# One-hots of the dot attention's edges made during propagation, in halves, beside those of its nodes

## The chip, the cores and the metric

The kernel runs on one core of a Trainium2 chip. The time is that of one execution on the device, in microseconds (us). Engines are called as in the profile: PE (TensorE, matrix products; PEld is its weight load), DVE (VectorE), ACT (ScalarE), POOL (GpSimd) and SP (SyncE, which here only issues DMAs). ACT issues DMAs too.

## What is computed

Four graph layers over one graph of 3125 nodes with 96 features and 50000 edges, each fed with a layer norm and a ReLU and added to x. Cut to what matters:

```python
edge_index = jnp.stack([src, dst])
h = relu(layernorm(x))
x = x + L0(h, edge_index)      # propagation, K = 10: out = spmm(out) * 0.9 + h * 0.1
h = relu(layernorm(x))
x = x + L1(h, W, ...)          # graph attention (softmax over the edges of a node)
h = relu(layernorm(x))
x = x + L2(h, qW, kW, vW, src, dst)   # dot attention
h = relu(layernorm(x))
x = x + L3(h, edge_index, W, b)       # mean of neighbours, projected

# L0: out[row] = sum over edges of out[col] / sqrt(deg_row * deg_col), ten times
# L2, the dot attention, heads = 4:
q = (embeds[rows] @ qW); k = (embeds[cols] @ kW); v = (embeds[cols] @ vW)
scores = clip(sum over a head's features of q * k, -10, 10)
w = exp(scores) / (sum of exp over the edges of a row + 1e-8)
res = segment_sum(w * v, rows)
```

## The kernel before

Nodes lie in 25 tiles of 128 (`TILES`, padded length `NPAD` = 3200). Edges are bucketed by (tile of the source, tile of the target), and one bucket of 128 slots holds each pair, so 25 x 25 buckets are gone through once (one round).

**Stages.** `build_counts` counts the edges into a 25 x 25 matrix of 128 x 128 blocks (`count16`, on chip) and writes the edges' ids to DRAM in several layouts: `ids_dram` (slot by slot), `by_src` and `by_dst` (rows of ids). `propagate` is L0, `graph_attention` L1, `dot_attention` L2, `mean_aggregate` L3. They run one after the other, with a barrier between blocks.

**Propagation.** Ten turns (`K_STEPS`). In a turn, PE makes 25 sums (one for each tile i), each of 25 products of 128 x 128 by 128 x 192 (L1248), into five banks in rotation (`BANKS`). DVE turns each sum into the next turn's operand with the four instructions of `update` (L1171, L1173, L1175, L1177) and counts `y_ready` up. PE may start the sum of tile i + 5 when tile i has been updated, and the first sum of a turn needs the last tile of the turn before only for its last product. Before, `update` keeps its 32-bit result in `y32`, a quarter of the tensor `work`.

**Node one-hots on the side.** The dot attention gathers and scatters by matrix products with one-hot matrices. Those of the edges' source and target *within their tile's row of ids* (SRC and DST, "node one-hots", 2 x 25 of 128 x 3200 in f16) are made during propagation: 100 halves of 128 x 1600. For each, SP broadcasts a row of ids to all 128 partitions (L1029), DVE compares it in place with the partition's number (L1035), and ACT stores it to the DRAM tensor `hot_by_src` (L1040). There are three buffers in x. DVE makes one after the updates of tiles 1, 3, ..., 19 of each turn (`SPOT_AFTER`). After every fourth half SP also writes a tile of `count16` to DRAM (L1196).

**The dot attention's loop.** 25 steps s (source tiles), each of three groups of 10, 10 and 5 buckets, numbered j = 0 to 74. Each engine runs a program of its own, in a fixed order, and semaphores tie them together. Per group j, PE gathers q and k (`gather`, L1852 and L1853), the v of group j-1, and scatters group j-3 (L1881, L1882). k has one place in PSUM, so PE may gather the next k only when DVE's product of this one (L1941) is done. DVE does the product (L1941), the weighted value of group j-1 (L1948), which waits for ACT's three instructions of the weight of that group (L1906, L1908, L1910), and the reduction (L1954). Behind the reduction of a step's second group stands `spot_edges(s + 1)` (L1926): one instruction over 128 x 3200 that makes the next step's edge one-hot, the scatter matrix, from a table of slot ids (`cols`), and behind it `add` (L1932). SP loads the two node one-hots of step s three steps ahead (L1756), waiting for `q_done` and `v_done`.

## Time and profile before

| | us |
|---|---|
| median of 3 runs | 1625.02 (1624.86 to 1630.6) |
| profiled execution, its own time | 1627.73 |
| its span, first to last instruction | 1625.9 |
| DVE busy / PE busy / ACT busy / POOL busy | 1259.8 / 1237.4 / 546.2 / 373.9 |
| propagation, first to last sum | 324.65 to 859 |
| dot attention's loop, first to last product (L1941) | 1252.8 to 1518.0 |

The busy share of an engine over the whole span says little here, since stages with different limits follow each other: in the 40 slices of the page PE stands at 9 tenths through propagation with DVE at 5 to 8, and in the dot attention's slices DVE stands at 9 with PE at 8. The views that matter are the sums over a stretch and the timeline of one step. A row of the timeline gives the start, the duration, and in brackets how long the engine had been idle before it and what ended that. Two instructions that follow each other on DVE overlap by up to 0.1 us in their records, so what one costs is read from start to start.

### The profile page before, as it was taken

To read this page: it belongs to the slowest core of one execution; us is meant where nothing else is said; L and a number is where in the kernel's file an instruction comes from. 1 tells how busy PE (TensorE), PEld (TensorE's weight loads), DVE (VectorE), ACT (ScalarE), POOL (GpSimd) and SP (SyncE) were. 2 spreads that over 40 slices of the span, in tenths; PEclk is the share of its full clock that TensorE was granted. 3 is DMA by queue.
4 is the path that set the end of the run, shared out by engine and by line. 5 is a ranking of instruction groups with operands and counts; after the bars stand their busy time and mean duration, and the time that the engine had idled before them with its cause. 6 is when DMAs were issued, how large, how long until landed. Compare 5 with 4: busy or idle time off the path is not lost. (4 is left out here: it accounts for less than half of the span.)

```text
span 1625.9 us, 44876 instructions
## 1 busy us (share of the span) xinstructions
PE 1237.4 (76%) x18543; PEld 1174.0 (72%) x18544; DVE 1259.8 (77%) x2302; ACT 546.2 (34%) x1096; POOL 373.9 (23%) x211
## 2 busy tenths in 40 slices
PE   4767777399999999999994004888856888888468
PEld 3356767399899999999993004787755887888368
DVE  7888888766566565665667998999988999999733
ACT  0047777400000000000002873333335777777311
POOL 1400000000000000000001012888862665656300
PEclk6858777699999999999997556999997999999789
DMA  0012222375475565654563683555513444543293
GB/s 10 0 46 109 105 103 109 109 249 190 151 240 204 161 196 194 213 194 164 203 213 110 225 298 123 204 201 189 200 68 117 144 159 149 164 146 122 96 343 101
DMA packets 74936, 256.85 MB, mean 158 GB/s; under 512 B 17999, under 2 KB 19576, under 8 KB 74732
## 3 DMA queue, kind: packets, MB, share of 16 engines
q1 hardware_dynamic: 59996, 211.70, 38.6%
q10 hardware_dynamic: 14400, 40.97, 6.5%
q8 instruction: 160, 2.62, 0.7%
q0 software_dynamic: 336, 1.20, 0.3%
q14 instruction: 44, 0.36, 0.1%
HBM read 168.15 MB, written 85.68 MB: 156 GB/s over the span
## 5 line engine op out<-in xcount | busy, mean ns | idle before, releaser
L1248 PE MATMUL psum<-work,count 128*128 128x192 f16 x6250 | 521.4, 247 | 30.7 <-issue 30.7
L1248 PEld LDWEIGHTS psum<-work,count 128*128 128x128 f16 x6250 | 519.7, 98 | 32.5 <-issue 31.8
L1171 DVE SCALAR_TENSOR_TENSOR work<-psum,small,work 128x96 f32<-128x96 f32 x250 | 79.5, 318 | 177.4 <-PE psum L1248 177.3
L1585 PE MATMUL psum<-count 128*128 128x98 f16 x625 | 113.1, 209 | 134.5 <-DVE count L1632 98.2
L1852 PE MATMUL psum<-count 128*128 128x100 f16 (+1 forms) x1875 | 181.4, 207 | 44.5 <-DVE count L1941 30.7
L1852 PEld LDWEIGHTS psum<-count 128*128 128x128 f16 x1875 | 162.7, 98 | 55.3 <-issue 36.0
L929 ACT ACTIVATE work<-work 128x1248 f32<-128x1248 f32 (+1 forms) x6 | 7.2, 1203 | 576.9 <-DVE work L912 576.8
L1917 POOL TENSOR_TENSOR count<-count 128x1000 bf16<-128x1000 f32 (+1 forms) x75 | 160.8, 2143 | 122.0 <-ACT count L1901 122.0
L1624 POOL TENSOR_TENSOR count<-count 128x970 bf16<-128x970 f32 (+1 forms) x75 | 166.7, 2236 | 91.2 <-ACT count L1617 91.2
L1853 PE MATMUL psum<-count 128*128 128x100 f16 (+1 forms) x1875 | 180.8, 207 | 0.0
L1853 PEld LDWEIGHTS psum<-count 128*128 128x128 f16 x1875 | 164.4, 98 | 0.0
L1585 PEld LDWEIGHTS psum<-count 128*128 128x128 f16 x625 | 61.1, 98 | 141.1 <-DVE count L1632 98.4
L1214 POOL MEMSET x<- 128x96 f32 x1 | 0.2, 178 | 562.0 <-DMA onehots_by_src<-x 562.0
L1586 PE MATMUL psum<-count 128*128 128x98 f16 x625 | 112.9, 208 | 0.0
L1588 PE MATMUL psum<-count 128*128 128x98 f16 x625 | 112.8, 208 | 0.0
L1587 PE MATMUL psum<-count 128*128 128x98 f16 x625 | 112.7, 208 | 0.0
L1617 ACT CAST count<-count 128x970 f16<-128x970 f32 (+1 forms) x75 | 64.9, 867 | 110.3 <-DVE count L1668 110.3
L1536 DVE CUSTOM_DVE_ANT_0 count<-count 128x3200 bf16<-128x3200 f32 x25 | 91.0, 3641 | 4.8 <-ACT count L1386 0.8
L728 ACT ACTIVATE count<-psum 128x512 f32 (+3 forms) x175 | 92.8, 547 | 1.2 <-PE psum L458 1.2
L1632 DVE TENSOR_SCALAR count<-count,small 128x3200 f16<-128x3200 f16 x50 | 89.0, 1783 | 0.7 <-PEq L1484 0.7
L1173 DVE SCALAR_TENSOR_TENSOR work<-psum,small,work 128x96 f32<-128x96 f32 x250 | 79.4, 317 | 8.8
L2176 PE MATMUL psum<-count 128*128 128x194 f16 x625 | 58.4, 250 | 31.3 <-issue 31.3
(286 smaller groups left out, 2695.7 us busy)
## 6 DMA issues: line engine op xcount, KB each, us to landing
x<-bucket_rows_by_src SPq DMA_DIRECT2D x100, 400.0 KB, 4.6
onehots_by_src<-x ACTq DMA_DIRECT2D x100, 400.0 KB, 4.3
count<-bucket_rows_by_dst SPq DMA_DIRECT2D x50, 800.0 KB, 4.4
count<-onehots_by_src SPq DMA_DIRECT2D x50, 800.0 KB, 4.3
count_f<-count SPq DMA_DIRECT2D x25, 800.0 KB, 6.8
count<-count_turned SPq DMA_DIRECT2D x25, 800.0 KB, 5.8
count<-count_f SPq DMA_DIRECT2D x17, 800.0 KB, 4.3
count_turned<-x SPq DMA_DIRECT2D x25, 416.0 KB, 2.4
```

What stands on the lines that cost most here:

```text
L728: nc.scalar.activation(count16[:, bass.ds(t, 1), b0 * P:(b0 + n) * P], ps[:, at * CH:at * CH + n * P].unsqueeze(1), ACT.Copy, accum_out=in ...
L1248: last = nc.tensor.matmul(bank[i % BANKS], count16[:, j, i * P:(i + 1) * P], y[par][:, j, :], start=(j == 0), stop=(j == TILES - 1))
L1536: nc.vector.tensor_tensor_reduce(bent, asrc, masks[t % 2], 1.0, -3e38, ALU.subtract, ALU.max, top[:, t:t + 1]).then_inc(topped, 1)
L1585: nc.tensor.matmul(ps[:, at:at + GW], node_hot[SRC][t % 2][:, s, :], high[:, s, :], start=True, stop=False, skip_group_check=True)
L1586: nc.tensor.matmul(ps[:, at:at + GW], node_hot[SRC][t % 2][:, s, :], low[:, s, :], start=False, stop=False, skip_group_check=True)
L1587: nc.tensor.matmul(ps[:, at:at + GW], node_hot[DST][t % 2][:, s, :], wide_high[:, t, :], start=False, stop=False, skip_group_check=True)
L1588: last = nc.tensor.matmul(ps[:, at:at + GW], node_hot[DST][t % 2][:, s, :], wide_low[:, t, :], start=False, stop=True, skip_group_check=True)
L1624: nc.gpsimd.tensor_tensor(value_low[i % (LAG + 1)][:, 0:n * EW], value[i % RING][:, 0:n * EW], value_high[i % (LAG + 1)][:, 0:n * EW], ALU ...
L1632: nc.vector.tensor_scalar(node_hot[v][t % 2].rearrange("p t n -> p (t n)"), spread[v][t % 2], small[:, 504:505], None, ALU.is_equal).then_ ...
L1852: nc.tensor.matmul(slot(b, i, width), hot[:, t0 + i, :], high[:, of, at:at + width], start=True, stop=False, skip_group_check=True)
L1853: last = nc.tensor.matmul(slot(b, i, width), hot[:, t0 + i, :], low[:, of, at:at + width], start=False, stop=True, skip_group_check=True)
L1917: nc.gpsimd.tensor_tensor(value_low[i % 3][:, 0:n * VW], value[i % 2][:, 0:n * VW], value_high[i % 3][:, 0:n * VW], ALU.subtract).then_inc ...
```

## The change

The edge one-hots are no longer made inside the dot attention. They are made in propagation too, as 50 halves of 13 and 12 tiles (128 x 1664 and 128 x 1536), stored to DRAM behind the node one-hots (`hot_by_src` grows from 50 to 75 rows), and loaded from there in the dot attention as a third 800 KB load per step. So propagation has 150 pieces (`PIECES`), in the order node, edge, node (`piece % 3 == 1` is an edge piece), and they are made in the first nine turns: after the updates of tiles 1 to 20, in five of every six places. Node halves have four buffers in place of three, the fourth in the memory of `y32`; edge pieces have one, there too, and so an edge compare waits for the store of the edge piece before it. `update` keeps its 32-bit result in two small buffers (`passing`) but in the last turn, where it goes to `y32` as before. The table of slot ids is loaded once at propagation's start, only its source half (128 x 25 runs of 50 ids), ahead of the first node half on SP's queue, and POOL makes the row of numbers that it is compared with. Eleven semaphores of `build_counts` are cleared and given back to make room. The `cols` tensor and its load go from the dot attention.

```diff
-    spots, HALVES = m["spots"], BY_SRC_HALVES
-    SPOT_AFTER = range(1, 21, 2)
-    halves = [view(m["x"], i * HALF_ROW // 2, HALF_ROW, F16) for i in range(3)]
+    spots, steps_space, x_space = m["spots"], Space(m["work"][:, 3 * W:4 * W]), Space(m["x"])
+    node_halves = [x_space.take(HALF_ROW, F16) for _ in range(NODE_BUFFERS - 1)] + [steps_space.take(HALF_ROW, F16)]
+    pieces = Pieces(node_halves, steps_space.take(HALF_TILES[0][1] * P, F16), steps_space.take(2 * TILES * TILES, F16), view(m["small"], 160, P, F16))
+    passing = [steps_space.take(D), m["work"][:, 4 * W + P:4 * W + P + D]]
+    LAST = K_STEPS - 1
...
-            spots.loads(sp, halves, half_row, HALVES, store_count_tile)
+            spots.load_ids(sp, pieces, 0, ids_dram)
+            for n in range(NODE_HALVES):
+                spots.load(sp, pieces, 0, n, by_src)
+                store_count_tile(n)
...
                 for turn in range(K_STEPS):
+                    if turn == LAST:
+                        spots.wait_stored(dve)
                     for i in range(TILES):
-                        update(dve, turn * TILES + i, bank[i % BANKS], at_tile(i), y[1 - turn % 2])
-                        if i in SPOT_AFTER:
-                            spots.compare(dve, halves, turn * len(SPOT_AFTER) + SPOT_AFTER.index(i))
+                        update(dve, turn * TILES + i, bank[i % BANKS], at_tile(i), y[1 - turn % 2], y32[:, i, :] if turn == LAST else passing[i % 2])
+                        q = 20 * turn + i - 1
+                        if turn < LAST and 1 <= i <= 20 and q % 6 < 5:
+                            spots.compare(dve, pieces, 5 * (q // 6) + q % 6)
...
+    def compare_edges(self, dve, pieces, e):
+        s, half = divmod(e, 2)
+        t0, t1 = HALF_TILES[half]
+        if e == 0:
+            dve.wait_ge(self.counted, 1)
+            dve.wait_ge(self.ids_loaded, 16)
+        else:
+            dve.wait_ge(self.edges_stored, 16 * e)
+        shape = [P, t1 - t0, P // 2, 2]
+        self.nc.vector.tensor_tensor(pieces.edge[:, 0:(t1 - t0) * P].rearrange("p (t n d) -> p t n d", n=P // 2, d=2),
...
             def _(sp):
                 for s in range(3, TILES):
-                    for v, done in ((SRC, "q_done"), (DST, "v_done")):
+                    for v, done in ((SRC, "q_done"), (DST, "v_done"), (EDGE, "scattered")):
                         sp.wait_ge(S[done], (s - 2) * PER)
                         load_hot(sp, s, v)
...
-                            pe.wait_ge(S["edge_hot"], s + 1)
+                            pe.wait_ge(S["hot_%d%d" % (EDGE, s % 3)], 16 * (s // 3 + 1))
...
-                        if s + 1 < TILES:
-                            if t0 == GROUP:
-                                spot_edges(s + 1)
```

How the instructions stand now. DVE in the middle of a step of the dot attention's loop, from the product of its second group on, before:

```order
L1941 TENSOR_TENSOR count<-psum,count 128x960 [waits dot_reduced,dot_q_copied,dot_k_done]
L1948 TENSOR_TENSOR count<-psum,count 128x1000 [waits slots_low_done,slots_exped,dot_v_done]
L1954 TENSOR_REDUCE count<-count 128x40 [waits dot_multiplied]
L1926 TENSOR_TENSOR count<-work,count 128x3200 [waits slots_scattered]
L1932 TENSOR_TENSOR count<-count,psum 128x100 [waits slots_scattered]
L1941 TENSOR_TENSOR count<-psum,count 128x480 [waits dot_reduced,dot_q_copied,dot_k_done]
L1948 TENSOR_TENSOR count<-psum,count 128x1000 [waits slots_low_done,slots_exped,dot_v_done]
```

and in the changed kernel, where L1984, L1991, L1997 and L1976 are the product, the value, the reduction and the add:

```order
L1984 TENSOR_TENSOR count<-psum,count 128x960 [waits dot_reduced,dot_q_copied,dot_k_done]
L1991 TENSOR_TENSOR count<-psum,count 128x1000 [waits slots_low_done,slots_exped,dot_v_done]
L1997 TENSOR_REDUCE count<-count 128x40 [waits dot_multiplied]
L1976 TENSOR_TENSOR count<-count,psum 128x100 [waits slots_scattered]
L1984 TENSOR_TENSOR count<-psum,count 128x480 [waits dot_reduced,dot_q_copied,dot_k_done]
L1991 TENSOR_TENSOR count<-psum,count 128x1000 [waits slots_low_done,slots_exped,dot_v_done]
```

The one instruction between the reduction and the add is gone; nothing else has moved. DVE in propagation, a stretch of a middle turn, before (a node compare behind every second update):

```order
L1035 TENSOR_SCALAR x<-x,small 128x1600 [waits spot_half_loaded_1]
L1171 SCALAR_TENSOR_TENSOR work<-psum,small,work 128x96 [waits step_tile_summed]
L1173 SCALAR_TENSOR_TENSOR work<-psum,small,work 128x96 [waits y_tile_steps]
L1175 CAST work<-work 128x96 [waits y_tile_steps]
L1177 TENSOR_TENSOR work<-work 128x96 [waits y_tile_steps]
L1171 SCALAR_TENSOR_TENSOR work<-psum,small,work 128x96 [waits step_tile_summed]
L1173 SCALAR_TENSOR_TENSOR work<-psum,small,work 128x96 [waits y_tile_steps]
L1175 CAST work<-work 128x96 [waits y_tile_steps]
L1177 TENSOR_TENSOR work<-work 128x96 [waits y_tile_steps]
L1035 TENSOR_SCALAR x<-x,small 128x1600 [waits spot_half_loaded_2]
```

and in the changed kernel (L1074 is the edge compare, L1063 the node compare, L1217 to L1223 the update):

```order
L1223 TENSOR_TENSOR work<-work 128x96 [waits y_tile_steps]
L1074 TENSOR_TENSOR work<-small,work 128x1664 [waits edge_half_stored]
L1217 SCALAR_TENSOR_TENSOR work<-psum,small,work 128x96 [waits step_tile_summed]
L1219 SCALAR_TENSOR_TENSOR work<-psum,small,work 128x96 [waits y_tile_steps]
L1221 CAST work<-work 128x96 [waits y_tile_steps]
L1223 TENSOR_TENSOR work<-work 128x96 [waits y_tile_steps]
L1063 TENSOR_SCALAR x<-x,small 128x1600 [waits node_half_loaded_1]
L1217 SCALAR_TENSOR_TENSOR work<-psum,small,work 128x96 [waits step_tile_summed]
```

A piece now stands behind nearly every update, and one in three of them waits for a store. SP's queue at the start of propagation in the changed kernel:

```order
L1048 DMA work<-bucket_ids 128x25x50
L1055 DMA x<-bucket_rows_by_src 128x1600 x3
L1055 DMA work<-bucket_rows_by_src 128x1600
L1242 DMA count_f<-count 128x3200
L1055 DMA x<-bucket_rows_by_src 128x1600 [waits node_half_stored_0]
```

where before the first was a load of a node half; the id table is now ahead of it.

## Rows read from the trace of the kernel before

**Rows 1.** Stretches: length; PE, PEld, DVE, ACT, POOL busy; PE clock; DMA share; GB/s.

```profile
325.00:859.00 534.00, 521.07 (x6249) 519.35 (x6247) 330.03 (x1097) 0.00 (x0) 0.18 (x1) 0.99 0.59 198
1252.80:1518.00 265.20, 224.89 (x4895) 214.66 (x4894) 253.81 (x268) 189.74 (x367) 155.78 (x73) 1.00 0.43 139
```

**Rows 2.** Timeline of DVE, step 23 of the loop and what follows: start, duration.

```profile
1500.55 1.16 DVE L1941 TENSOR_TENSOR count<-psum,count 128x960 f32<-128x960 f32 x1
...
1505.96 1.14 DVE L1954 TENSOR_REDUCE count<-count 128x40 f32<-128x960 f32 x1
1507.02 1.82 DVE L1926 TENSOR_TENSOR count<-work,count 128x3200 f16<-128x3200 f16 x1
1508.75 0.25 DVE L1932 TENSOR_TENSOR count<-count,psum 128x100 f32<-128x100 f32 x1
1508.92 0.65 DVE L1941 TENSOR_TENSOR count<-psum,count 128x480 f32<-128x480 f32 x1
1509.49 1.19 DVE L1948 TENSOR_TENSOR count<-psum,count 128x1000 f32<-128x1000 f32 x1
...
1511.37 1.16 DVE L1941 TENSOR_TENSOR count<-psum,count 128x960 f32<-128x960 f32 x1
```

**Rows 3.** The same view, last step, which has no edge compare.

```profile
1516.78 1.14 DVE L1954 TENSOR_REDUCE count<-count 128x40 f32<-128x960 f32 x1
1517.84 0.25 DVE L1932 TENSOR_TENSOR count<-count,psum 128x100 f32<-128x100 f32 x1
1518.05 0.66 DVE L1941 TENSOR_TENSOR count<-psum,count 128x480 f32<-128x480 f32 x1
1519.09 1.20 DVE L1948 TENSOR_TENSOR count<-psum,count 128x1000 f32<-128x1000 f32 x1 [0.39 <-ACT count L1910]
```

**Rows 4.** Who waited for whom in 1252.8 to 1518: us in total, times, longest.

```profile
PEld psum L1852 <- issue: 33.3, 24, 1.7
PEld psum L1852 <- DVE count L1948: 15.4, 41, 0.6
...
DVE count L1941 <- PE psum L1853: 1.2, 1, 1.2
```

**Rows 5.** Timeline of PE's weight loads: the last of the gather of k behind 1508.92.

```profile
1510.48 0.10 PEld L1853 LDWEIGHTS psum<-count 128*128 128x128 f16 x1
```

**Rows 6.** Timeline of DVE in the middle of a turn of propagation.

```profile
490.75 0.32 DVE L1171 SCALAR_TENSOR_TENSOR work<-psum,small,work 128x96 f32<-128x96 f32 x1 [0.85 <-PE psum L1248]
...
491.88 0.63 DVE L1035 TENSOR_SCALAR x<-x,small 128x1600 f16<-128x1600 f16 x1
492.81 0.32 DVE L1171 SCALAR_TENSOR_TENSOR work<-psum,small,work 128x96 f32<-128x96 f32 x1 [0.31 <-PE psum L1248]
```

**Rows 7.** Groups by shape, DVE: f16 comparisons of the build stage; busy us, mean ns.

```profile
L627 DVE TENSOR_TENSOR work<-work,x 128x1664 f16<-128x1664 f16 x25 | 25.4, 1017 | 0.0
```

**Rows 8.** View of line L1040, the 100 stores of node halves.

```profile
DMA to landing us min/median/max: 2.3/4.3/7.8
```

**Rows 9.** DMA issues: size, median us to landing.

```profile
x<-bucket_rows_by_src SPq DMA_DIRECT2D x100, 400.0 KB, 4.6
...
work<-in_x_dram POOLq DMA_DIRECT2D x1, 1152.0 KB, 8.6
...
bucket_ids<-x SPq DMA_DIRECT2D x25, 25.0 KB, 2.0
```

**Rows 10.** Stretches with the DMA engines near full, columns as in rows 1.

```profile
465.00:467.00 2.00, 2.00 (x27) 2.00 (x25) 1.59 (x6) 0.00 (x0) 0.00 (x0) 1.00 1.00 408
1214.00:1226.00 12.00, 0.00 (x0) 0.00 (x0) 11.82 (x10) 4.61 (x5) 0.00 (x0) 0.50 0.95 369
```

**Rows 11.** Timeline of DVE at the start of propagation.

```profile
330.62 0.32 DVE L1171 SCALAR_TENSOR_TENSOR work<-psum,small,work 128x96 f32<-128x96 f32 x1 [0.85 <-PE psum L1248]
...
333.67 0.64 DVE L1035 TENSOR_SCALAR x<-x,small 128x1600 f16<-128x1600 f16 x1 [1.84 <-DMA x<-bucket_rows_by_src]
334.22 0.31 DVE L1171 SCALAR_TENSOR_TENSOR work<-psum,small,work 128x96 f32<-128x96 f32 x1
```

More of the change, by code:

```diff
@@ L933, in _, with spot_next_round @@
             scalar_after(act)
-def spot_next_round(nc, m, halves, row, hot, n):
+def spot_next_round(nc, m, pieces, k, ids_dram, by_src, hot_by_src):
     spots = m["spots"]
@@ L941, in _, with many @@
         def _(sp):
-            if_one(sp, m, None, lambda: spots.loads(sp, halves, row, n))
+            def many():
+                spots.load_ids(sp, pieces, k, ids_dram)
+                for n in range(NODE_HALVES):
+                    spots.load(sp, pieces, k, n, by_src)
+            if_one(sp, m, None, many)
         @block.vector
@@ L946, in many @@
             def many():
-                for i in range(n):
-                    spots.compare(dve, halves, i)
+                dve.sem_inc(spots.counted, 1)
+                for piece in range(PIECES):
+                    spots.compare(dve, pieces, piece)
             if_one(dve, m, None, many)
@@ new lines, in load, with compare @@
+    def load(self, sp, pieces, k, n, by_src):
+        if n >= NODE_BUFFERS:
+            sp.wait_ge(self.stored[n % NODE_BUFFERS], 16 * (n // NODE_BUFFERS))
+        w, half = divmod(n, 2)
+        row = by_src[bass.ds(k, 1), w].rearrange("k t n -> k (t n)")[:, half * HALF_ROW:(half + 1) * HALF_ROW]
+        sp.dma_start(pieces.node[n % NODE_BUFFERS], row.broadcast_to([P, HALF_ROW])).then_inc(self.loaded[n % NODE_BUFFERS], 16)
+    def compare(self, dve, pieces, piece):
+        if piece % 3 == 1:
+            self.compare_edges(dve, pieces, piece // 3)
+        else:
+            n = self.node_of(piece)
+            dve.wait_ge(self.loaded[n % NODE_BUFFERS], 16 * (n // NODE_BUFFERS + 1))
+            self.nc.vector.tensor_scalar(pieces.node[n % NODE_BUFFERS], pieces.node[n % NODE_BUFFERS], self.partition, None, ALU.is_equal).then_inc(self.made, 1)
@@ new lines, in stores @@
+    def stores(self, act, pieces, hot_by_src):
+        for piece in range(PIECES):
+            act.wait_ge(self.made, piece + 1)
+            if piece % 3 == 1:
+                s, half = divmod(piece // 3, 2)
+                t0, t1 = HALF_TILES[half]
+                act.dma_start(hot_by_src[:, 2 * TILES + s, t0 * P:t1 * P], pieces.edge[:, 0:(t1 - t0) * P]).then_inc(self.edges_stored, 16)
+            else:
+                n = self.node_of(piece)
+                w, half = divmod(n, 2)
+                act.dma_start(hot_by_src[:, w, half * HALF_ROW:(half + 1) * HALF_ROW], pieces.node[n % NODE_BUFFERS]).then_inc(self.stored[n % NODE_BUFFERS], 16)
@@ L1217, in _ @@
         def _(act):
-            spots.stores(act, halves, half_hot, HALVES)
+            spots.stores(act, pieces, hot_by_src)
         @block.tensor
@@ L1255, in large @@
             def large():
-                for i in range(HALVES):
-                    spots.compare(dve, halves, i)
+                for piece in range(PIECES):
+                    spots.compare(dve, pieces, piece)
+                spots.wait_stored(dve)
                 with dve.Fori(0, K_STEPS // 2) as kk:
```

127 lines of the change are left out of this document (61 added, 66 removed).

## The prediction

> **What bounds the kernel now.** I read first the sums over two stretches, propagation and the dot attention's loop, since the change takes work from one and puts it in the other [rows 1]. In propagation PE is busy 521 of 534 us and DVE 330: PE sets the time. In the loop DVE is busy 254 of 265 us, PE 225, ACT 190, POOL 156: DVE sets it. Then the timeline of one step [rows 2]: it runs from 1500.55 to 1511.37, 10.82 us, and DVE is hardly idle in it. One instruction of it, the edge compare, holds DVE from 1507.02 to 1508.75, 1.73 us from start to start [rows 2].
>
> **The loop, without the edge compare.** It can't give back 1.73 us a step, because it hides a wait. The weighted value of the second group needs ACT's three weight instructions, which start when the reduction at 1505.96 ends, and they are done long before 1509.49 only because the compare lies between. What happens without it is in this trace: the last step has no edge compare [rows 3]. From the reduction (1516.78) to the weighted value (1519.09) it takes 2.31 us, 0.39 of them spent waiting for ACT. With the compare it takes 1509.49 - 1505.96 = 3.53 us [rows 2]. So a step gives back 3.53 - 2.31 = 1.22 us. Behind the weighted value nothing changes in DVE's order, so the next product stands 1511.37 - 1509.49 = 1.88 us behind it as before, if PE has the next k by then, and the step becomes 9.60 us.
>
> PE has it. The third product, at 1508.92 today, 2.96 us behind the reduction, comes 1.27 behind it in the last step [rows 2, 3]. PE gathers the next k when it is done, and has waited for that 33.3 us in 24 steps, 1.39 each [rows 4]. So this gather can start 1.39 us earlier, and it is needed only 1.22 earlier; besides, its last weights are loaded at 1510.48 and the product that needs it starts at 1511.37 [rows 5, 2], some 0.7 us later even with 0.2 for its last matmul. Together the margin is 0.17 + 0.7 = some 0.9 us. On busy time the others have room: PE 224.9 / 265.2 x 10.82 = 9.2 us a step, ACT 7.7, POOL 6.4, against 9.60.
>
> There are 25 edge compares. The first stands ahead of the first product, where DVE then waits 1.2 us for PE anyway [rows 4]; I give it nothing. The other 24 lie in steps 0 to 23: **24 x 1.22 = 29.3 us**. The bounds are 0 and the whole of the instruction, 24 x 1.73 = 41.5 us. I take 29.3, since rows 3 are the very order of instructions that the changed kernel has.
>
> **The third load per step.** SP loads 3 x 0.82 MB in 9.60 us, 256 GB/s, and the DMA engines have moved 369 GB/s at 0.95 of their time with such loads [rows 10]. SP now also waits for the scatter of step s-3 before it goes on to the load of step s+1, which moves that load from early in its step to near its end; it is needed two steps, 19 us, later. Cost: nothing, hidden behind two steps; without that cover, one landing of some 4 to 7 us, once. Nine loads stand ahead of the loop in place of six, which were under way from 1214 on [rows 10]; three more at 369 GB/s are 6.7 us, over long before 1252.8.
>
> **Propagation, DVE's time.** An update with the piece behind it takes, start to start, 491.88 - 490.75 = 1.13 us for the update [rows 6] and 0.55 for a node compare (333.67 to 334.22) [rows 11]. An edge half is an f16 comparison of two tensors; the nearest row has just its shape, 1.02 us [rows 7], less the overlap of 0.08 that the node compare shows (0.63 against 0.55): 0.94. PE delivers a sum every 492.81 - 490.75 = 2.06 us. So a node place leaves 0.38 us, an edge place -0.01, an empty one 0.93. Over six places (3.33 nodes, 1.67 edges, one empty) DVE needs 10.2 of 12.4 us. It keeps up, and in tiles 21 to 24, with no piece, it can work off 4 x 0.93 = 3.7 us. At a turn's end the last update is needed by the last product of PE's next sum, 2.06 us after its sum is ready, and takes 1.13 plus handoffs, so some 0.6 us may be left over: 4.3 us in all. In the middle of a turn PE is five tiles ahead, and DVE may be 4 x 2.06 - 1.13, less 0.2 of handoffs, some 6.9 us late before PE waits. **Cost: 0.**
>
> **Propagation, the edge store that DVE now waits for.** An edge compare waits for the store of the edge half before. Queued behind that wait are DVE's updates, and behind these PE. 50 edge pieces in 180 places are 3.6 places or 7.4 us apart (3 places, 6.2 us, at the least). Less the compare and 0.1 of handoffs, a store may take 5.2 us in the close pairs and 6.4 us on the mean. The stores of today take 2.3 to 7.8, 4.3 in the median [rows 8]. So some edge compares will wait a us or two, within the 4.3 and 6.9 us above. The node halves have four buffers and 14.9 us for a round of load, compare and store; 4.6 + 0.6 + 4.3 [rows 9, 8] fit. **Cost: 0 at today's landings.** But these will be longer: in 18 places (37.1 us) the queues now carry 25 halves of 0.41 MB and 2.5 count tiles of 0.82 MB, 12.3 MB or 331 GB/s, against 20 and 2.5 in 41.3 us before, 248. The trace has moved 408 GB/s, loads and stores mixed, over two us in this very stage [rows 10], so 331 is 0.81 of that, and I expect the store's median at 5, still free.
>
> The Trainium skill speaks against this: its page "DMA: Bandwidth & Descriptors", section "Where 436 GB/s comes from", puts the limit for transfers between HBM and SBUF at about 358 GB/s per core. By it the new load would fill 0.92 of what there is, and the sum would lean to rival 1 below, with a time between 1600 and 1617. The rows do not bear the limit out for short stretches (408, and 369 over 12 us), and the measurement decides.
>
> **Propagation, the start.** The id table stands in the queue ahead of the first node half, for which DVE waits to 333.67 already, 1.84 us [rows 11]. It is 3200 runs of 100 bytes. Nearest rows: 128 runs of 200 bytes land in 2.0 us, 3072 runs of 384 bytes (from POOL's queue) in 8.6 [rows 9]. So it adds between 0 (a DMA more can't speed up the one behind it) and 6.6 us; I take 3. DVE is then 1.5 + 3 = 4.5 us late at the update of tile 2, under 6.9, and hidden by PE's five banks; at 6.6 it would be 8.1, and PE would lose 1.2 us. Taken: 0.
>
> **The rest.** POOL's row of numbers and the clearing of semaphores lie on an idle POOL beside longer DVE work; `passing` changes addresses only; the stores end in the ninth turn, so the last turn's wait for them is met, and the load of x that follows comes earlier, a gain that I take as 0.
>
> **Sum.** The profiled execution took 1627.7 us, span 1625.9 and 1.8 around it. Span after: 1625.9 - 29.3 = 1596.6, time 1598.4. That execution lies 2.7 above the median 1625.0; on the median's footing 1625.0 - 29.3 = **1595.7 us**.
>
> **Rivals.**
> 1. *The store sets DVE's pace.* If stores land in L us on the mean, DVE falls behind by L - 6.4 per edge piece, 5.6 times a turn, and 4.3 are worked off: PE loses 9 x (5.6 x (L - 6.4) - 4.3). That is nothing to L = 7.2, 17 us at 7.5, and all of the 29.3 at L = 7.75; at L = 8 it is 42, and the kernel would take 1638. For it: 331 GB/s, landings up to 7.8 today. Against it: the median of 4.3, and 408 GB/s moved. A part given back (1600 to 1617): 0.15. All of it and more, the case that ends slower: 0.05; within 0.5% of before: 0.02.
> 2. *PE's gather of k comes late in the loop.* It decides from a delay of 0.9 us on, and each 0.1 us beyond costs 2.4 us. If PE paced the loop with its busy 9.2 us and its other wait (15.4 / 24 = 0.6 [rows 4]), the step would be 9.8 us and the gain 24 x 1.0 = 24: 1601; with some more for a late third load 1608. Chance 0.06.
> 3. *The loop gives back the whole instruction*, if ACT's weights come sooner than in the last step: 1625.0 - 41.5 = 1583.5, at the least 1590. Against it are rows 3. Chance 0.06.
>
> **How the numbers follow.** The forecast, 1590 to 1600, has 0.66. Under 1588 lie some 0.05, over 1608 some 0.15 (half of rival 1's first case, and its others), so 1588 to 1608 holds 0.8; it takes in the start's 1.2 us. A measurement of this kernel can tell about 0.5%, 8.1 us. Faster by more than that: 0.66 + 0.15 + 0.06 + 0.06 = 0.93, less a little at 1617, 0.92. Same 0.03, slower 0.05.
>
> **What would show it.** In the profile after: a step of the loop of 9.60 us, with a wait of 0.4 us for ACT before the weighted value in every step; PE's wait named "issue" in the loop near nothing; the loop 29 us shorter. Propagation from first to last sum as long as before, with PE at 0.98 and waits of DVE for the edge store, a few of them, below 3 us; store landings of about 5 us; the first node compare some 3 us later. Wrong would be PE pausing at turn ends, landings over 7 us, or a step over 9.8 us.

## The result, and what the profile after shows

| | before | after |
|---|---|---|
| median, us | 1625.93 (1624.86 to 1630.6, 4 runs) | 1612.99 (1610.39 to 1615.28, 4 runs) |
| ratio of the two | | 0.9912, 95% interval 0.9892 to 0.9933 |
| profiled execution, its span | 1625.9 | 1613.4 |

The changed kernel is 0.9% faster, 13 us. The prediction said 1595.7, between 1588 and 1608: the sign was right, and 17 us of the gain did not come. The two spans differ by 12.5 us, and read stretch by stretch they add up so:

| stretch | before | after | difference |
|---|---|---|---|
| start to propagation's first product | 324.65 | 326.08 | +1.4 |
| propagation, to its last product | 534.0 | 547.7 | +13.7 |
| from there to the first product of dot attention's loop | 394.1 | 394.0 | -0.1 |
| the loop, first to last product | 265.2 | 237.5 | -27.7 |
| from there to the end | 107.85 | 108.1 | +0.25 |

The 1.4 us at the start can't be put down to the change: kernels with one and the same code up to there start propagation at 324.2 (e7, below) and 326.1 (after). So the loop gave nearly what was forecast, and propagation gave half of it back. The sums over the two stretches of after, columns as in [rows 1]:

```profile
326.10:873.80 547.70, 526.03 (x6250) 523.47 (x6250) 370.49 (x1146) 0.00 (x0) 0.18 (x1) 0.98 0.64 231
1267.80:1505.30 237.50, 221.50 (x4896) 213.89 (x4895) 215.97 (x245) 189.70 (x367) 127.86 (x73) 1.00 0.62 231
```

**The loop.** DVE is busy 216.0 us in it instead of 253.8. The timeline of DVE over one step of after (start, duration, idle time and what ended it); the weighted value (L1991) at 1381.17 waits 0.39 us for ACT, just as in the step that stood for it [rows 3], and comes again at 1390.80, 9.63 us later:

```profile
1381.17 1.20 DVE L1991 TENSOR_TENSOR count<-psum,count 128x1000 f32<-128x1000 f32 x1 [0.39 <-ACT count L1963]
...
1389.75 0.66 DVE L1984 TENSOR_TENSOR count<-psum,count 128x480 f32<-128x480 f32 x1
1390.80 1.20 DVE L1991 TENSOR_TENSOR count<-psum,count 128x1000 f32<-128x1000 f32 x1 [0.39 <-ACT count L1963]
```

Who waited for whom in the loop: first the wait of DVE for ACT before, then two rows of after. Beside the short wait of 0.2 us a step that was there before, the one of 0.39 us a step has appeared (4.8 us in 24 times became 14.3 in 48), PE's weight loads wait 22.2 us for DVE's value instead of 15.4 [rows 4], and the 33.3 us that PE had waited for "issue" have no row any more:

```profile
DVE count L1948 <- ACT count L1910: 4.8, 24, 0.2
...
PEld psum L1905 <- DVE count L1991: 22.2, 48, 0.7
...
DVE count L1991 <- ACT count L1963: 14.3, 48, 0.5
```

**Propagation.** Here one row of the page's list of groups says where to look: PE's products, busy time, mean ns of one, and the idle time just before them. Before:

```profile
L1248 PE MATMUL psum<-work,count 128*128 128x192 f16 x6250 | 521.4, 247 | 30.7 <-issue 30.7
```

And after:

```profile
L1298 PE MATMUL psum<-work,count 128*128 128x192 f16 x6250 | 526.1, 248 | 39.6 <-issue 38.3
```

Of the idle time 18.1 us before and 17.9 after are the wait before the first product. The rest is 12.6 us before and 21.7 after, and but for 1.3 us of it, in after, no other engine is named for it. The timeline of PE shows where it stands. Before, at the first two of the four places where PE's loop over laps of two turns (`pe.Fori(0, K_STEPS // 2)`) jumps back:

```profile
433.20 2.13 PE L1248 MATMUL psum<-work,count 128*128 128x192 f16 x16 [3.62 <-issue]
...
540.59 1.57 PE L1248 MATMUL psum<-work,count 128*128 128x192 f16 x17 [2.44 <-issue]
```

After, at the same two places, and at the one place where PE waited for DVE:

```profile
381.83 0.26 PE L1298 MATMUL psum<-work,count 128*128 128x192 f16 x1 [0.43 <-DVE work L1223]
382.95 1.25 PE L1298 MATMUL psum<-work,count 128*128 128x192 f16 x13 [0.86 <-DVE work L1223]
...
438.07 2.26 PE L1298 MATMUL psum<-work,count 128*128 128x192 f16 x13 [5.36 <-issue]
...
548.44 1.78 PE L1298 MATMUL psum<-work,count 128*128 128x192 f16 x10 [5.08 <-issue]
```

Before the third pause of the kernel before (PE's last product starts at 643.64), this is what moved in the 4 us from 639.6 (queue, packets, MB, share of the 16 engines):

```profile
q1 hardware_dynamic: 190, 0.52, 34.9%
q8 instruction: 2, 0.03, 4.8%
```

In after, in the 4 us ahead of the same pause (648.9 to 652.9):

```profile
DMA packets 413, 1.32 MB, mean 330 GB/s; under 512 B 48, under 2 KB 48, under 8 KB 412
...
q1 hardware_dynamic: 281, 0.94, 59.0%
```

And in the pause itself (653 to 657.6):

```profile
q1 hardware_dynamic: 189, 0.52, 35.5%
q8 instruction: 2, 0.03, 2.8%
```

Before, both packets were under way before PE had run out of work. After, in a stretch in which the engines move 330 GB/s, neither had started, and both came when PE already stood still. The Trainium skill has the rule that this fits (page "Runtime: NRT & Kernel Launch", section "Instruction fetch mechanics"): instructions come in 16 KB blocks by DMA, the fetch ahead is purely sequential, and a taken branch to a block that isn't there stalls the engine until it is fetched. It gives no duration. The trace agrees: each pause has its two packets of 16 KB, and it ends behind them.

The trace holds each packet's own start and end, of which the view gives sums. The later packet of a pair lands 0.9 to 1.8 us behind PE's last product before, and 2.9 to 3.9 us behind it in after. PE goes on 1.5 to 1.9 us later in the one, and 1.5 to 1.6 us later in the other. The same holds at all 32 jumps back in the eight profiles of kernels that keep PE's loop, here and below: 1.5 to 2.2 us from that landing to PE's next product, 1.5 to 1.7 in 25 of them. So what makes one pause longer than another is, nearly all of it, how late the second packet lands. DVE is not it: its last update of a lap ends 1.2 us behind PE's last product at every one of the four jumps, in before and in after alike, and every pause lasts longer than that.

A long enough pause costs twice. Stretches of 3 us that begin some 0.6 us behind the first two pauses (length, PE busy and products, granted clock, DMA share, GB/s), before and after:

```profile
433.80:436.80 3.00, 3.00 (x22) 0.51 0.00 0
541.20:544.20 3.00, 3.00 (x39) 1.00 0.00 0
```

```profile
438.70:441.70 3.00, 3.00 (x21) 0.50 0.08 30
549.10:552.10 3.00, 3.00 (x25) 0.61 0.00 0
```

Behind the pauses of 3.62 and 3.45 us PE ran at 1.2 GHz for some 3.4 us (22 products in 3 us of it, for 39 at 2.4 GHz); behind those of 2.44 and 3.11 it went on at 2.4. In after it fell behind all four. Interval by interval, what PE's 6250 products take over 82.5 ns each (the mean from start to start at 2.4 GHz) is 18.3 us before and 32.0 after: pauses 13.3 and 21.0, low clock 5.0 and 9.3 (1.7 of it at propagation's start in both), lateness of DVE 0 and 1.6. The difference is the 13.7 us.

**Theories.** A: PE's pauses are the loading of its own instructions at the back jump, over the DMA engines that carry the one-hots; the change put more data ahead of it there. B: DVE is late, for want of its loads and of the edge store, as rival 1 of the prediction had it. C: something else in the changed kernel's code.

### The profile page after: what moved, and what is told of

Read it like the earlier page. It is cut to its first block and busy times, and to the rows that moved or that the text cites. A ratio compares the mean times of both kernels' runs of the same rounds, so it can differ in the third digit from the quotient of the medians.

```text
span 1613.4 us, 44985 instructions
## 1 busy us (share of the span) xinstructions
PE 1244.6 (77%) x18543; PEld 1182.5 (73%) x18544; DVE 1260.8 (78%) x2327; ACT 546.3 (34%) x1096; POOL 346.3 (21%) x212
## 5 line engine op out<-in xcount | busy, mean ns | idle before, releaser
L1905 PE MATMUL psum<-count 128*128 128x100 f16 (+1 forms) x1875 | 179.1, 207 | 20.2 <-DVE count L1991 17.2
L1217 DVE SCALAR_TENSOR_TENSOR work<-psum,small,work 128x96 f32<-128x96 f32 x250 | 79.3, 317 | 127.1 <-PE psum L1298 126.8
L1906 PE MATMUL psum<-count 128*128 128x100 f16 (+1 forms) x1875 | 178.6, 207 | 0.0
L1970 POOL TENSOR_TENSOR count<-count 128x1000 bf16<-128x1000 f32 (+1 forms) x75 | 133.1, 1774 | 121.9 <-ACT count L1954 121.9
L1991 DVE TENSOR_TENSOR count<-psum,count 128x1000 f32<-128x1000 f32 (+1 forms) x75 | 76.7, 1023 | 16.2 <-ACT count L1963 14.7
```

Of the source, the lines that this page charges most:

```text
L1905: nc.tensor.matmul(slot(b, i, width), hot[:, t0 + i, :], high[:, of, at:at + width], start=True, stop=False, skip_group_check=True)
L1906: last = nc.tensor.matmul(slot(b, i, width), hot[:, t0 + i, :], low[:, of, at:at + width], start=False, stop=True, skip_group_check=True)
L1970: nc.gpsimd.tensor_tensor(value_low[i % 3][:, 0:n * VW], value[i % 2][:, 0:n * VW], value_high[i % 3][:, 0:n * VW], ALU.subtract).then_inc ...
```

## The experiments

Medians are of 4 or 5 runs each, of 2 in e8 and in the second look at e1, beside 7 runs of the kernel before on the same chip (medians 1627.0 for e1, e3, e4 and e5; 1627.6 for e6, e8, e9 and the second look; 1627.5 for e7 and e10). Each row of products shown carries a wait of 17.7 to 18.4 us ahead of the first one.

### e1: the places of the kernel before, four tiles later

```diff
-    SPOT_AFTER = range(1, 21, 2)
+    SPOT_AFTER = range(5, 25, 2)
```

> The kernel before, with its node compares moved four tiles later in each turn (behind the updates of tiles 5, 7, ..., 23 in place of 1, 3, ..., 19). Same instructions, same DMAs, same bytes; but their DMAs are now under way when PE's loop of two turns (L1248) comes to its end and jumps back. Theory A (the pause of PE at the end of each lap is the loading of its instructions, which goes over the same 16 DMA engines and is slowed by data DMAs under way; a longer pause is followed by half clock): the four pauses grow from 2.6 to 3.8 us each to about 5, the products behind each run at half clock for some 3.3 us, propagation grows by 8 to 13 us, the time goes from 1626 to 1634 to 1639. Theory B (DVE's added work or the edge store's wait makes PE wait at the turn's end): nothing of it is here, no change, 1626 +- 3. Theory C (something else in the changed kernel, such as the fourth buffer or the id table): no change.

Measured: 1642.95 us, ratio 1.0097 (1.008 to 1.0115). The run that was profiled was the odd one of five, 1631.74. Its pauses were short (2.57 to 3.04 us) although the DMA engines were at 0.57 to 0.72 in the 4 us ahead of them. Theories B and C expected no change, and A 1634 to 1639, so all three missed the time. Busy engines alone don't lengthen a pause: a miss for theory A in its first form. And a cost that no theory had: the stores end later, so the load of x does, and the first product of the stage behind waits for it 22.65 us, where it had waited 13.31:

```profile
876.49 0.39 PE L1407 MATMUL psum<-ident,work 96*96 96x96 f32 x1 [22.65 <-DMA work<-in_L_gnn_bias_dram]
```

So the same kernel was run and profiled again:

> The kernel of e1 once more, for a profile of a typical run: four of its five runs took 1642 to 1644 us, and the one profiled 1632. Theory A in its sharper form expects the 11 us in PE's pauses at the lap ends (4.5 us and more, with half clock behind them, where the profiled run had 2.6 to 2.9), with a DMA share above 0.72 in the 4 us before them. Theory B expects them in PE's waits for VectorE in the tiles, with VectorE waiting for its stores.

Measured: 1643.55 us, and this time the profile was of a typical run. Its row of products, what DVE waited for its data in propagation, and its longest pause in the timeline:

```profile
L1248 PE MATMUL psum<-work,count 128*128 128x192 f16 x6250 | 525.8, 248 | 34.0 <-issue 34.0
```

```profile
DVE x L1035 <- DMA x<-bucket_rows_by_src: 1.3, 5, 0.4
```

```profile
545.59 2.65 PE L1248 MATMUL psum<-work,count 128*128 128x192 f16 x16 [4.90 <-issue]
```

Pauses of 3.93, 4.90, 3.04 and 4.12 us, with low clock behind all four, are +3.4 us of pause and +4.4 of clock against the kernel before; the late x adds 8.2 (21.52 for 13.31). Together 16, which is the loss. DVE waits for its data 1.3 us in all, so theory B has nothing here. The DMA share ahead of the four pauses was 0.87, 0.66, 0.62 and 0.91, and the longest pause stands behind 0.66: a mean share over 4 us orders the pauses roughly and not one by one. In that pause the first packet started 1.8 us before PE's last product and the second only 2.4 us behind it.

### e3 and e4: PE's turns written out, in the kernel before and in the changed one

```diff
-                with pe.Fori(0, K_STEPS // 2) as kk:
+                for kk in range(K_STEPS // 2):
```

> The kernel before, with PE's ten turns of propagation written out in place of a loop of five laps, so that PE never jumps back; all waits as before. Theory A: the four pauses (13.3 us in all) and the half clock behind two of them (3.3 us) vanish, propagation takes 534 - 16.6 = 517 us, the time about 1609. Theory B: the pause is PE waiting for DVE's last update, which is as late as before, so the pauses stay and the time is 1626.

> The changed kernel, with PE's ten turns written out in place of the loop. Theory A: the pauses (21.0 us) and the half clock behind them (7.6 us) vanish, only the waits for DVE in the first lap (1.6 us) stay; propagation takes 547.7 - 28.6 = 519 us, the time about 1613 - 28.6 = 1584, some 25 to 29 us below the straight kernel before. Theory B: DVE is behind at the turns' ends, the pauses stay as waits for DVE, 1610 to 1613.

Measured: e3 1618.11 us, ratio 0.9941 (0.9923 to 0.9958); e4 1590.18 us, ratio 0.977 (0.9753 to 0.9787). The row of products in e3, and then in e4:

```profile
L1248 PE MATMUL psum<-work,count 128*128 128x192 f16 x6250 | 517.6, 246 | 17.7 <-issue 17.7
```

```profile
L1298 PE MATMUL psum<-work,count 128*128 128x192 f16 x6250 | 519.6, 247 | 20.1 <-issue 17.7
```

Nothing is left of PE's pauses but the wait before the first product and, in e4, 2.4 us for DVE at 380.8 to 383.7. Propagation's products take 517.6 us from first to last in e3 (534 before) and some 522 in e4 (547.7). The page's row of the instruction queue q8 has 152 packets in both, for 160 with the loop: two fewer for each of the four jumps. The packets that remain in propagation are hidden: from 425 to 436, where the kernel before had paused, e3's PE is busy all the time (the stretch, and the instruction queue's row in the DMA view of it):

```profile
425.00:436.00 11.00, 11.00 (x136) 11.00 (x134) 6.02 (x22) 0.00 (x0) 0.00 (x0) 1.00 0.28 98
```

```profile
q8 instruction: 1, 0.02, 0.6%
```

Between e3 and e4, neither of which has pauses, stands the change itself: 27.9 us, the whole gain of the loop. That is what the changed kernel would have given if propagation had really been free. What theories B and C could still name is at most 4.5 us, DVE's lateness in e4's profiled execution with the low clock behind it.

Both came out slower than expected, e3 by 9 us and e4 by 6. In e3 1.6 us of it lie ahead of the first product. In both, 6 us lie in the last stage (113.7 and 114.1 us from the loop's last product to the end, for 107.85 and 108.1 with PE's loop). Two products into it, e4's PE pauses (timeline), while the engines are full and one instruction packet comes (DMA view of the pause):

```profile
1516.93 0.50 PE L2216 MATMUL psum<-count 128*128 128x194 f16 x2 [31.10 <-issue]
1522.44 6.47 PE L2216 MATMUL psum<-count 128*128 128x194 f16 x48 [5.01 <-issue]
```

```profile
DMA packets 352, 2.01 MB, mean 410 GB/s; under 512 B 40, under 2 KB 40, under 8 KB 351
...
q8 instruction: 1, 0.02, 1.4%
```

The changed kernel with its loop has no such pause there. Written-out turns shift all code behind them, so this looked like a block's edge that had moved to a bad place; e9 puts that to the test. The packet lands 1.3 us before PE goes on, much as at the jumps.

### e5: no pieces near the ends of laps, PE's loop kept

```diff
-                        q = 20 * turn + i - 1
-                        if turn < LAST and 1 <= i <= 20 and q % 6 < 5:
-                            spots.compare(dve, pieces, 5 * (q // 6) + q % 6)
+                        if (turn, i) in piece_at:   # tiles 1 to 15 of odd turns, 1 to 23 of even ones, 6 of 7
+                            spots.compare(dve, pieces, piece_at[turn, i])
```

> The changed kernel, its loop kept, with the same 150 pieces at other places: in the turns that end a lap of PE's loop none behind tile 15, in the others up to tile 23. Same work and bytes, but quiet DMA engines at the laps' ends. Theory A: the pauses go back to 2.6 to 3.8 us and half of the half clock goes, propagation 537 to 540, the time 1602 to 1606. Theory B: DVE has no more slack than before the move, no change or slower, 1610 to 1616.

Measured: 1606.19 us, ratio 0.9864 (0.9843 to 0.9884). PE's program is that of the changed kernel. Ahead of the first lap's end the engines are at rest (stretch); the shares ahead of the other three are 0.36, 0.04 and 0.04. The pauses are short again, 2.46, 2.20, 2.17 and 2.43 us for 4.45 to 5.47. The records of the second and third name DVE's last update as what ended them, but it was done 0.9 to 1.0 us before PE went on, and the second packet had landed 1.5 to 1.6 us before, as everywhere:

```profile
431.70:435.70 4.00, 4.00 (x52) 4.00 (x49) 2.21 (x8) 0.00 (x0) 0.00 (x0) 1.00 0.01 4
```

```profile
438.40 1.87 PE L1300 MATMUL psum<-work,count 128*128 128x192 f16 x14 [2.46 <-issue]
...
549.84 2.40 PE L1300 MATMUL psum<-work,count 128*128 128x192 f16 x27 [2.20 <-DVE work L1225]
```

It also shows theory B's mechanism at work where places are packed closer: DVE waits 30.1 us for the edge store (13.2 in after), and PE 10.9 us for DVE, 4.4 of them those two lap ends:

```profile
DVE work L1074 <- DMA onehots_by_src<-work: 30.1, 13, 3.2
...
PE psum L1300 <- DVE work L1225: 10.9, 6, 2.5
```

So B is a real cost in this variant, and 1.6 us in the changed kernel. Against after, propagation gains 11.1 us of pause and 0.5 of clock and loses 5.5 to DVE: 6.1 us in the profile, and the medians differ by 6.8. The time is 0.2 us beyond the range of theory A and well under that of B. Some 2.4 us remain at each of the three lap ends with the engines at rest.

### e6 and e7: each half of the change alone

e6 has the propagation of the kernel before and the loop of the changed one; e7 the reverse. e6 leaves out the making of edge one-hots altogether: its third load takes rows of node one-hots, of the same size, so its result is not the reference's.

```diff
e6, against the kernel before:
-            for v in (SRC, DST):
+            for v in (SRC, DST, EDGE):
...
-                            if t0 == GROUP:
-                                spot_edges(s + 1)
e7, against the changed kernel: the same lines the other way round
```

> The propagation of the kernel before (two thirds of the one-hots, its places and its stores) with the dot attention of the changed kernel: three loads a step and no compare of edges on VectorE. The third load takes rows that hold node one-hots, so the values are not the reference's. All theories expect the loop's gain alone: 27.8 us less from the loop's first product to its last, propagation as in the kernel before (534 us, its pauses at the lap ends 2.4 to 3.6 us), so about 1598 us. If it came out above 1603, the loop would give less by itself than in the changed kernel, and propagation would not be the only place that gave back.

> The other half of e6: the changed kernel's propagation, with all 150 pieces made and stored and PE's turns in their loop, and the dot attention of the kernel before, which loads two rows a step and makes the edge one-hot itself on VectorE. Theory A expects what the changed kernel's propagation cost, and nothing else: pauses of 4.5 us and more at the lap ends with half clock behind, the stretch from propagation's first product to its last 547 us instead of 534, and the loop as in the kernel before (265.2 us from first product to last): 1627 + 13.7 + 1.4 for the start = about 1642 us. Were the cost tied to the third load of the loop or to the new loop's code, this kernel would stand at 1627 to 1630.

Measured: e6 1598.56 us, ratio 0.9825 (0.9801 to 0.985); e7 1640.78 us, ratio 1.0092 (1.0066 to 1.0118). Sums over propagation and the loop, e6 and then e7:

```profile
326.00:857.40 531.40, 519.93 (x6250) 518.47 (x6250) 329.85 (x1096) 0.00 (x0) 0.18 (x1) 0.99 0.60 199
1251.60:1488.70 237.10, 221.47 (x4897) 213.71 (x4895) 216.00 (x245) 190.29 (x367) 127.91 (x73) 1.00 0.63 231
```

```profile
324.20:865.20 541.00, 524.53 (x6250) 522.45 (x6250) 370.36 (x1146) 0.00 (x0) 0.18 (x1) 0.98 0.66 234
1258.90:1524.50 265.60, 225.27 (x4895) 215.06 (x4894) 253.91 (x268) 189.75 (x367) 155.76 (x73) 1.00 0.43 138
```

The halves add: -29.0 and +13.3 us make -15.7, against -13 for both together, which is near enough for runs of one kernel that lie 5 to 10 us apart. By e6's profile the loop with its third load gives 28.1 us by itself (from first to last product, 237.1 for 265.2), and by the medians making the pieces costs 13. e7's profiled execution was the shortest of its four (1634.3; the others 1638 to 1644): its propagation took 541 us, 7 more than before, and its pauses were 3.81, 2.54, 4.13 and 5.99. The length of a pause differs from run to run of one kernel, as in e1.

### e8: the kernel before, with copies beside it as a lap ends

```diff
+            for lap in range(1, K_STEPS // 2):
+                if lap > 1:
+                    pool.wait_ge(beside, 64 * (lap - 1))
+                pool.wait_ge(summed, 2 * TILES * lap - 3)
+                for c in range(4):
+                    pool.dma_start(m["beside"][c:c + 1], by_dst[0:1]).then_inc(beside, 16)
```

> The kernel before with one thing added: after tile 47 of every second turn, some 6 us before PE's lap of two turns ends, GpSimd issues four copies from DRAM to DRAM of 320 KB each, 1.28 MB in all, four times in propagation. VectorE's steps, their places and their stores stay as they are. Theory A in its sharper form (PE's pause at the back jump is the loading of its instructions over the same DMA engines, and grows where these have a backlog as the lap ends: a share of 0.75 to 0.87 in the last 4 us gave 4.5 to 5.5 us, 0 to 0.72 gave 2.2 to 3.6): the four pauses grow from 2.4 to 3.6 us to 4.5 or more, with half clock behind each, 8 to 14 us in all: 1633 to 1640 us. Theory B (lateness of VectorE for want of loads and stores) expects the pauses as before and, if anything, waits of PE for VectorE in the tiles after them, 0 to 5 us. Theory C (something else in the changed kernel's code): no change, 1625.

Measured: 1643.49 us, ratio 1.0105 (1.0083 to 1.0126), 3 us beyond what A expected. The row of products, and the longest pause:

```profile
L1256 PE MATMUL psum<-work,count 128*128 128x192 f16 x6250 | 525.5, 248 | 40.2 <-issue 40.2
```

```profile
657.61 1.62 PE L1256 MATMUL psum<-work,count 128*128 128x192 f16 x9 [6.57 <-issue]
```

The pauses are 4.63, 5.41, 6.57 and 5.17 us, with low clock behind all four, and propagation is 13.2 us longer, which is what the change did to it. Nothing of the change is in this kernel, PE's program is the same, and PE never waits for DVE. In the 4 us ahead of the longest pause (stretch from 646.8) the engines carry copies and one-hots, and there is no row of the instruction queue. The sum of the DMA view over these 4 us:

```profile
DMA packets 249, 1.17 MB, mean 293 GB/s; under 512 B 46, under 2 KB 46, under 8 KB 218
```

In the pause (650.9 to 657.6) the copies are q0, and what moves beside them is little:

```profile
q0 software_dynamic: 72, 0.60, 21.2%
q8 instruction: 2, 0.03, 3.6%
q1 hardware_dynamic: 7, 0.01, 0.3%
```

Both instruction packets start only 2.4 us after PE has stopped, among the last of the copies, and the second lands 2.0 us later; 2.1 us behind that PE goes on.

Theory A is shown in both directions: less traffic ahead of the jump shortens the pauses (e5), more of it lengthens them (e8), no jump removes them (e3, e4), and every pause ends at its own distance of 1.5 to 2.2 us behind the second packet. C falls with e5, where the changed kernel's other code has short pauses, and with e8, which has long ones without it.

### e9 and e10: two steps further

```diff
e9, against e4:
-            if_one(pe, m, lambda: one_tensor(pe), lambda: tensor_program(pe, F32))
+            def many():                             # the branch that isn't taken here
+                tensor_program(pe, F32)
+                for _ in range(24):
+                    pe.sem_inc(filler, 1)
+            if_one(pe, m, lambda: one_tensor(pe), many)
e10, against e9:
-            spots.load_ids(sp, pieces, 0, ids_dram)
             for n in range(NODE_HALVES):
                 spots.load(sp, pieces, 0, n, by_src)
+                if n == 0:
+                    spots.load_ids(sp, pieces, 0, ids_dram)
...
+    places = [(0, i) for i in range(2, 22, 2)] + [(turn, i) for turn in range(1, LAST) for i in range(1, 22)]
```

> The changed kernel with PE's ten turns written out (as e4, 1590.2 us), and 24 instructions more in a branch of the last stage that isn't taken here, so that the code behind it lies 24 instructions further on. In e4 PE stops for 5.0 us two products into the last stage, a pause that the changed kernel with its loop hasn't. If that is one more loading of instructions, which comes where the code crosses from one loaded piece into the next, it moves away: the last stage takes 108 to 109 us from the loop's last product to the end instead of 114.1, about 1585 us. If the pause has another cause (the load of the first tile, the clock), it stays: 1590.

> e9 (written-out turns, 24 instructions of filler; 1587.0 us) with the pieces given out otherwise: ten in the first turn, at every second tile, and 140 in the other eight turns, at tiles 1 to 21, five of every six; and the id table is loaded behind the first node half instead of ahead of it, so that the first node compare has its row earlier (it waited 4.4 us in the changed kernel, 0 to 3 expected here). By theory A there is no more to be had than what PE lost in e9 to VectorE and clock, 2.3 us at its cold start in the profiled run and up to 4.5 more in e4's: 1583 to 1588 us. By theory B VectorE's lateness in the first lap costs in the runs without a profile too: 1582 to 1584.

Measured: e9 1586.95 us, ratio 0.9755 (0.9739 to 0.9771); e10 1583.9 us (1583.65 to 1584.02), ratio 0.9735 (0.9718 to 0.9753), 2.6% less than the kernel before and 29 us less than the changed one. The start of e9's last stage (timeline), to set beside e4's:

```profile
1516.68 5.98 PE L2216 MATMUL psum<-count 128*128 128x194 f16 x50 [31.12 <-issue]
```

24 instructions that are never executed removed a pause of 5 us: a packet lands at the same distance behind the stage's first product as in e4 (4.3 and 4.2 us), and PE is at work then. From the loop's last product to the end it takes 108.0 us, for 114.1 in e4. The medians differ by 3.2 only. e4's profiled execution was the slowest of its four (1593.5, the others 1589.0 to 1590.3), so what e4 lost in the last stage in the others isn't known. In e10 the first node compare has its row at once (DVE's timeline), where after waited 4.42 us for it, and PE's row of products has nothing left:

```profile
333.94 0.63 DVE L1063 TENSOR_SCALAR x<-x,small 128x1600 f16<-128x1600 f16 x1
```

```profile
L1301 PE MATMUL psum<-work,count 128*128 128x192 f16 x6250 | 517.9, 247 | 18.0 <-issue 18.0
```

e9's profile has no wait of PE for DVE either, although DVE waited 21.1 us for the edge store and 13.3 for its loads there. So which of e10's two edits gave its 3 us, and in which runs, stays open.

## Why the prediction was wrong, point by point

**The loop: right in mechanism, 1.6 us too large.** 24 x 1.22 = 29.3 was the term; the first-to-last product gave 27.7. The step is 9.63 for 9.60, 0.03 us in each of the other 22. The rest is missing in the first two steps: the first went from 9.90 us to 8.88 (1252.83 to 1262.73, and 1267.82 to 1276.70), so it gave 1.0, and the second, with a new wait of 0.50 for a reduction, gave 0.7 (10.65 to 9.99). PE's k was never late (rival 2), and the bound of 41.5 (rival 3) was as far off as rows 3 said. The third load cost nothing, as forecast: with it e6's steps are 9.63 us too.

**Propagation, DVE's time and the edge store: right, near enough.** "Keeps up, cost 0" was 1.3 us of waiting and 0.3 us about it. The landings moved as forecast: stores of node halves, and then of edge halves, in after:

```profile
DMA to landing us min/median/max: 2.3/5.6/9.5
...
DMA to landing us min/median/max: 2.3/4.8/8.5
```

The forecast was a median of 5, and DVE's waits for the edge store were indeed few and below 3 us:

```profile
DVE work L1074 <- DMA onehots_by_src<-work: 13.2, 10, 2.2
DVE x L1063 <- DMA x<-bucket_rows_by_src: 12.7, 8, 4.4
```

The second row is that of the node halves' loads, which the prediction had as fitting their round: 4.4 of its 12.7 us are the first one's, and the rest is a small miss. What all of it costs in the changed kernel is 1.6 us of 13.7. Rival 1, which would have been the explanation at hand (a time of 1613 lies in its range), is not what happened.

**Propagation, the start: right.** The id table was priced at 3 us and cost 2.6: the first node compare comes at 337.73 for 333.67, and 1.4 of these 4.06 us are the later start of propagation; DVE waited 4.42 us for its row instead of 1.84. It was then 4.2 us late at the update of tile 2 (forecast 4.5), under the 6.9 that PE's banks hide. PE's 1.3 us of waiting stand at that turn's end, where the prediction allowed DVE 4.3 us. The late start was nearly worked off by then (0.9 us at tile 15); a wait of 3.18 us for a node half's load and one of 2.17 for the edge store came behind it, and DVE was 5.0 us late at tile 21. In e4's profile it was 6.3 late and PE waited 2.4 us, in e9's 3.4 late and in e10's not at all in that turn, and PE waited for nothing. So the bound of 4.3 holds in these four profiles, and landings broke it in the first turn, not the late start.

**The step that failed** is the first one: "In propagation PE is busy 521 of 534 us ... PE sets the time", and with it "Cost: 0", twice. PE sets the time, and 12.6 of its 534 us were idle. The text never asked what those were. They stood in the page as 30.7 us idle, ended by "issue", 12.6 more than the wait before the first product, in four pauses at PE's back jumps. Had they been looked at, the instruction packets beside them would have shown that PE's own program uses the DMA engines, and that the change's 331 GB/s touches the bounding engine too. Instead the traffic was priced only through DVE's waits. The prediction listed "PE pausing at turn ends" as what would show it wrong; it did pause there, for a cause that it hadn't thought of. In its place stands, by the runs: four pauses longer by 2 us each (7.7), low clock behind all four of them instead of two, and for longer (4.3), and 1.6 for DVE.

**The 358 GB/s of the Trainium skill** (page "DMA: Bandwidth & Descriptors", section "Where 436 GB/s comes from") was weighed against the change, and did not decide: propagation moved 231 GB/s on the mean in after, and e4 moved 410 GB/s over the 4.9 us of its pause. The section of the Trainium skill that did bear on the case, "Instruction fetch mechanics" (page "Runtime: NRT & Kernel Launch"), wasn't used.

**What stays open.** Why one run of a kernel has pauses of 2.6 to 3.0 us and the next of 3.0 to 4.9 (e1), beyond that the second packet lands late in the long ones (1.0 to 1.5 us behind PE's last product in the first look, 1.5 to 3.3 in the second); and why the share of the 4 us ahead doesn't order them. Where in the queues an instruction packet waits can't be seen in the trace.

## What to carry to other kernels

Before pricing what a change adds beside the bounding engine, account for that engine's own idle time to the last microsecond, "issue" above all: an idle time that no other engine owns may hang on a resource that the change is about to fill. Where a long body of PE instructions is looped only a few times, write it out, or keep the DMA queues empty for some microseconds ahead of the back jump. Undo or add one half at a time: here e6 and e7 gave the balance of the change in two runs, and e8 showed the cause without any of it.

## What the runs showed of the hardware

- A back jump of PE over a body of 1250 products cost 2.2 to 2.5 us in e5 (DMA share 0.01 to 0.04 in the 4 us ahead of three of them, 0.36 ahead of one), 2.4 to 3.6 in the kernel before (0.36 to 0.42), 4.5 to 6.6 in after and e8 (0.75 to 0.96). e7 does not fit that order: 3.8 us behind a full share, 6.0 behind 0.62. What fits all is the landing of the second instruction packet, 1.5 to 2.2 us before PE went on. Straight code of the same length cost nothing, with the engines at 0.28 (e3) and through the whole of e10's propagation.
- Behind each of the 14 such pauses of 3.8 us or more PE ran for some 3 us or longer at 1.2 GHz (after, e1's second look, e7, e8). Behind shorter ones it went either way: low behind 2.46 and 2.43 in e5, 3.04 in e1's second look, 3.48 in e6, 3.45 and 3.62 in the kernel before; at 2.4 GHz behind 2.20 and 2.17 in e5, all four of 2.57 to 3.04 in e1's first look, 3.11 in the kernel before, 3.58 in e6.
- Where the code behind a branch lies was worth 5 us of PE's time in the last stage (e4 and e9), with 24 instructions between the two cases.
